# Expert weights of a mixture-of-experts layer read in place at a register-held address

## The chip, the cores and the metric

One core of a Trainium2 chip. The metric is the device time in microseconds of one execution; less is better. Engines are named PE (TensorE), DVE (VectorE), ACT (ScalarE), POOL (GpSimd) and SP (SyncE); "ACTq", "SPq" and the like are their instruction streams (DMA issues, register and semaphore instructions).

## What is computed

A network of five stages over x of shape (32, 64, 16, 16): a positional term, a linear attention with a small convolution, a causal pooling over the batch, a mixture of experts, a second linear attention, a second mixture of experts. The change touches the two mixtures alone. Each takes 8192 tokens of 64 numbers:

```python
logits = einsum('bsd,de->bse', x, gate_w) + gate_b         # 16 experts
top_probs, top_idx = top_k(softmax(logits), 2)             # two per token, renormalised
h1 = einsum('bsd,edh->bseh', x, w1)                        # 64 -> 128, per expert
h2 = einsum('bsd,edh->bseh', x, w2)
hidden = silu(h1) * h2
expert_out = einsum('bseh,eho->bseo', hidden, w3)          # 128 -> 64
out = einsum('bseo,bse->bso', expert_out, dispatch)
```

All is float32. Matrix products are made of two terms, a value rounded to fp32r and the rest that the rounding leaves.

## The kernel before

The kernel computes only the two chosen experts of each token. Tokens are split into two parts (PARTS = 2) of 4096. For a part, the routing finds each token's two experts and a slot for each choice; slots are grouped in blocks of 256 (BS), and each block belongs to one expert. 24 units (NU) of two blocks (UNIT = 2) always hold them all. `owner` is a small integer tile in SBUF with the expert of each block. GpSimd scatters the tokens of a part to a DRAM buffer by slot (64 indirect DMAs, line 980) and later gathers the results (64, line 992).

All weights of all 16 experts lie in one SBUF tile, `WR` of [128, 16, 320] float32: per expert 128 columns of w1, 128 of w2, 64 of w3. Which expert a unit needs is known only at run time. So SP, for each unit, reads the two owners from `owner` into registers (line 964; one load of two numbers, each then checked against 0 and 15), and issues two DMAs that copy the two experts' [128, 320] from `WR` to a ring of four, `wb` (line 967). It may do so once VectorE has finished with that buffer (`w_lo`, four units before).

The loop over units is a software pipeline written out by hand (`steps`): eight units written out, twelve in a loop of four per turn whose index is in a register, the last four written out. Step n does on each engine, in this order:

- ScalarE: issue the load of unit n+4's tokens from DRAM into `xb` (line 1107); weights of n+3: wait for the fetched weights, copy `wb` to `wr[..., 0]`, rounded (line 1102, semaphore `w_hi`); tokens of n+3: copy the transposed tokens out of PSUM (line 1113); silu of n+2 (line 1118); halve n+1: round the hidden values (line 1124); issue the store of n-1's result (line 1128).
- VectorE: result of n-1 (reduction, line 1272); weights of n+3: wait for `w_hi`, subtract `wr[..., 0]` from `wb` to get the rest (line 1249, `w_lo`); product of n+2 (line 1256); rest of n+1 (line 1262).
- TensorE: transpose the tokens of n+3 (line 1033), the two up products of n+2 (line 1049), the down product of n (line 1060).

`xb`, `wb`, `wr` and `yb` are rings of four units; `xt`, `gate`, `hid`, `hh`, `hlo` and the PSUM banks are rings of two.

Around the loops: in the first mixture, both parts are routed, then GpSimd scatters part 0 and part 1, and after that gathers part 0. ScalarE starts the loop of part p when `scattered[p]` is full. After both loops VectorE combines part 0 (line 1309 and 1310); part 1's gather runs in the next stage. In the second mixture, part 0 was routed and scattered in the stage before; part 1 is routed first, then both loops run beside the scatter of part 1 and the gather of part 0. The last stage gathers part 1 and writes the output. Stages are separated by a barrier of all engines.

Of the kernel before, what the change touches and what calls it, by code (L numbers as in the profile page):

```python
# [16 lines left out]
F32 = mybir.dt.float32  # L17
# [7 lines left out]
P = 128  # L25
# [817 lines left out]
class Mixture:  # L843
# [53 lines left out]
    def blocks_room(self, st, sem, outlives):  # L897

        def sb(name, shape, dt=F32):
            return st.enter_context(self.nc.sbuf_tensor(self.L + name, shape, dt))  # L900

        def sems(*names):
            return [sem(self.L + n) for n in names]
        self.GY = [(outlives or st).enter_context(self.nc.sbuf_tensor(f"{self.L}gy{h}", [P, 2, TH, C], F32))
                   for h in range(PARTS - 1)] + self.GY[-1:]
        self.xb = sb("xb", [P, 4, 4, P])
        self.xt = sb("xt", [P, 2, UNIT * BS], F32R)
        self.wb = sb("wb", [P, 4, UNIT, WC])
        self.wr = sb("wr", [P, 4, 2, UNIT, WC], F32R)
        self.gate = sb("gate", [P, 2, UNIT * BS])  # L910
        self.hid = sb("hid", [P, 2, UNIT * BS])
        self.hh = sb("hh", [P, 2, UNIT * BS], F32R)
        self.hlo = sb("hlo", [P, 2, UNIT * BS], F32R)
        self.yb = sb("yb", [P, 4, 4 * C])
        self.own_v, = sems("ov")
        self.x_in, self.w_in, self.stored = (sems(*(f"{n}{j}" for j in range(4))) for n in ("xl", "wl", "ys"))
        self.turned, self.xt_out, self.up1, self.up2, self.down = sems("bt", "bx", "b1", "b2", "bd")
        self.w_hi, self.w_lo, self.silu, self.prod, self.h_hi, self.h_lo, self.y_out = sems(
            "wh", "wo", "si", "pr", "hh_", "ho", "yo")
# [36 lines left out]
                     ).then_inc(self.g_loaded, 16)  # L956

    def sync(self, sp):
        for part in range(PARTS):
            def fetch(n, j, i):  # L960

                self.free(sp, self.w_lo, part, n, 4)
                owners = self.owner[0:1, part, bass.ds(n, 1)].rearrange("p n b -> p (n b)")
                _, experts = self.nc.values_load_multi_w_load_instructions(
                    owners, engines=[mybir.EngineType.SP], min_val=0, max_val=E - 1)
                for b in range(UNIT):
                    sp.dma_start(self.wb[:, j, b:b + 1], self.WR[:, bass.ds(experts[b], 1)]).then_inc(self.w_in[j], 16)
            sp.wait_ge(self.owned, part + 1)
            self.steps(sp, fetch)
        for j in range(4):  # L970

            sp.wait_ge(self.stored[j], 16 * PARTS * ((NU + 3 - j) // 4))

    def scatter(self, pool, part):

# [117 lines left out]
        act.wait_ge(self.exp_in, part + 1)  # L1093
        act.activation(self.mx[:, part, 3], self.mx[:, part, 2], ACT.Exp).then_inc(self.exp_out, 1)

    def scalar(self, act):
        ps = self.ps
        for part in range(PARTS):
            def weights(n, j, i):
                act.wait_ge(self.w_in[j % 4], UNIT * self.filled(part, j, i))  # L1100
                self.free(act, self.down, part, n, 4)
                act.copy(self.wr[:, j % 4, 0], self.wb[:, j % 4]).then_inc(self.w_hi, 1)  # L1102

            def load(n, j):

# [137 lines left out]
    def vector(self, dve, then):  # L1243
        ps = self.ps
        for part in range(PARTS):
            def weights(n, j):

                dve.wait_ge(self.w_hi, part * NU + n + 1)
                dve.tensor_tensor(self.wr[:, j % 4, 1], self.wb[:, j % 4], self.wr[:, j % 4, 0].bitcast(F32),  # L1249
                                  ALU.subtract).then_inc(self.w_lo, 1)  # L1250

            def product(n, j):
                dve.wait_ge(self.silu, part * NU + n + 1)
# [59 lines left out]
def stage_mixture(nc, sem, mix, first, ready, weights_in, outlives=None):  # L1313


    with ExitStack() as st:
# [6 lines left out]
        with nc.Block() as block:  # L1323
            @block.sync
            def _(sp):
                if not first:
                    mix.load_gate(sp)
                sp.wait_ge(*weights_in)
                mix.sync(sp)

            @block.gpsimd
            def _(pool):
                pool.wait_ge(*ready)
                for part in range(first, PARTS):
                    mix.scatter(pool, part)
                for part in range(PARTS - 1):
                    mix.gather(pool, part)

            @block.tensor
            def _(pe):  # L1340
                for part in range(first, PARTS):
                    mix.route_tensor(pe, part)
                mix.tensor(pe)

            @block.scalar
            def _(act):
                for part in range(first, PARTS):
                    mix.route_scalar(act, part)
                mix.scalar(act)

            @block.vector
            def _(dve):
                then = counter(dve, mix.own_v)
                for part in range(first, PARTS):
                    mix.route_vector(dve, then, part, (lambda: None) if part else (lambda: mix.split_gate(dve)))
                mix.vector(dve, then)
                if outlives is None:
                    for part in range(PARTS - 1):
                        mix.combine(dve, then, part)
# [448 lines left out]
```

## Time and profile before

| What | us |
|---|---|
| runs (three) | 1463.96, 1475.67, 1478.31 |
| median of the runs | 1475.67 |
| span of the profiled execution, first to last instruction | 1099.1 |
| PE busy in the span | 602.3 |
| DVE busy | 698.3 |
| POOL busy | 589.1 |
| ACT busy | 410.9 |
| mean granted TensorE clock | 0.753 |

The profile is one execution. Its page gives the span from the first to the last instruction, not the time of the whole execution; the runs' times hold what lies around the span too. A row of the timeline gives start, duration, engine, line, operation and tiles, and in brackets the idle time before it with what ended it. The four expert loops lie at about 364 to 440 and 451 to 530 us (first mixture), 824 to 909 and 921 to 998 us (second).

### The profile page before, as it was taken

What the parts mean: (1) busy time and instruction counts of PE and PEld (TensorE: products, weight loads), DVE (VectorE), ACT (ScalarE), POOL (GpSimd) and SP (SyncE); (2) the same over time, 40 slices, a digit from 0 to 9 for tenths busy, and PEclk for the clock granted to TensorE, in tenths of its full rate; (3) what the DMA queues carried; (4) which work ended last, traced back from release to release, by engine and by line L of the source; (5) the groups of instructions that cost most, each with busy time, mean ns of one, the idle gap of its engine ahead of it and who ended that gap; (6) DMA issues with size and microseconds to landing.
All of it is one profiled execution on the core that took longest, in us unless ns stands there. A gap on an engine that the chain in (4) does not pass through costs nothing. (4 is left out here: it accounts for less than half of the span.)

```text
span 1099.1 us, 12315 instructions
## 1 busy us (share of the span) xinstructions
PE 602.3 (55%) x3397; PEld 478.4 (44%) x3397; DVE 698.3 (64%) x1125; ACT 410.9 (37%) x688; POOL 589.1 (54%) x558
## 2 busy tenths in 40 slices
PE   2789776213310588477279841598155884783000
PEld 2774773213310587477144431244044774772000
DVE  6482474686670598478877589775458893885111
ACT  1454225131300576467224232143135773771000
POOL 0242141420777778777477600677205777775775
PEclk9979887555555799699679865698557996996555
DMA  3000991000211698688261100011104985882211
GB/s 106 7 1 1 207 354 25 0 1 0 94 46 52 198 292 243 198 249 241 57 103 24 24 1 0 38 46 53 53 22 147 299 259 185 261 250 62 55 35 38
DMA packets 126199, 118.91 MB, mean 108 GB/s; under 512 B 24917, under 2 KB 111525, under 8 KB 126147
## 3 DMA queue, kind: packets, MB, share of 16 engines
q1 hardware_dynamic: 56104, 54.93, 16.5%
q10 hardware_dynamic: 53659, 38.16, 11.9%
q0 software_dynamic: 16384, 25.20, 8.4%
q8 instruction: 23, 0.38, 0.1%
q14 instruction: 29, 0.24, 0.1%
HBM read 42.73 MB, written 44.04 MB: 79 GB/s over the span
## 5 line engine op out<-in xcount | busy, mean ns | idle before, releaser
L980 POOL DMA_INDIRECT blocks_x<-L_ffnmhl,L_ffnslot x192 | 198.5, 1034 | 162.9 <-DVE L_ffnslot L1233 105.0
L992 POOL DMA_INDIRECT gy_last<-blocks_y,L_ffnslot x128 | 129.7, 1013 | 57.0 <-issue 38.4
L992 POOL DMA_INDIRECT L_ffngy<-blocks_y,L_ffnslot x128 | 128.1, 1001 | 39.0 <-issue 39.0
L1033 PE MATMUL L_ffnps<-ident,L_ffnxb 128*128 128x128 f32 x384 | 65.5, 300 | 128.3 <-DMA L_ffnxb<-blocks_x 118.6
L1249 DVE TENSOR_TENSOR L_ffnwr<-L_ffnwb,L_ffnwr 128x640 fp32r<-128x640 f32 x96 | 79.2, 826 | 69.7 <-ACT L_ffnwr L1102 68.9
L1049 PE MATMUL L_ffnps<-L_ffnxt,L_ffnwr 128*128 128x256 f32 x768 | 118.3, 299 | 3.0 <-ACT L_ffngate L1118 2.4
L980 POOL DMA_INDIRECT blocks_x<-L_ffnlhl,L_ffnslot x64 | 66.3, 1036 | 82.3 <-DVE L_ffnslot L1233 63.1
L1102 ACT CAST L_ffnwr<-L_ffnwb 128x640 fp32r<-128x640 f32 x96 | 69.8, 727 | 108.5 <-issue 86.5
L1033 PEld LDWEIGHTS L_ffnps<-ident,L_ffnxb 128*128 128x128 f32 x384 | 44.7, 151 | 138.7 <-issue 107.8
L1049 PEld LDWEIGHTS L_ffnps<-L_ffnxt,L_ffnwr 128*128 128x128 f32 x768 | 101.4, 197 | 4.5 <-issue 3.2
L1060 PE MATMUL L_ffnps<-L_ffnwr,L_ffnhlo 128*128 128x128 f32 x384 | 92.8, 280 | 0.0
L1060 PE MATMUL L_ffnps<-L_ffnwr,L_ffnhh 128*128 128x128 f32 x384 | 88.6, 268 | 6.6 <-DVE L_ffnhlo L1262 6.2
L1256 DVE TENSOR_TENSOR L_ffnhid<-L_ffngate,L_ffnps 128x512 f32<-128x512 f32 x96 | 65.5, 686 | 34.4 <-ACT L_ffngate L1118 31.6
L1060 PEld LDWEIGHTS L_ffnps<-L_ffnwr,L_ffnhh 128*128 128x128 f32 x384 | 74.7, 195 | 8.7 <-issue 6.9
L1537 ACT CAST l_vh<-l_vg 128x512 fp32r<-128x512 f32 x64 | 39.6, 619 | 98.2 <-DVE l_vg L1597 98.2
L1060 PEld LDWEIGHTS L_ffnps<-L_ffnwr,L_ffnhlo 128*128 128x128 f32 x384 | 75.0, 195 | 0.0
L1113 ACT CAST L_ffnxt<-L_ffnps 128x512 fp32r<-128x512 f32 x96 | 56.2, 585 | 48.3 <-PE L_ffnps L1033 40.8
L1472 PE MATMUL l_ps<-l_xT,l_wv 128*128 128x512 f32 x128 | 71.7, 652 | 1.2
L1006 PE MATMUL L_ffnps<-ident,L_ffnmhl 128*128 128x128 f32 x96 | 22.5, 428 | 90.0 <-DVE L_ffnmhl L1175 66.6
L1272 DVE TENSOR_REDUCE L_ffnyb<-L_ffnps 128x256 f32<-128x512 f32 x96 | 65.8, 685 | 3.7 <-PE L_ffnps L1060 3.5
L1597 DVE SCALAR_TENSOR_TENSOR l_vg<-l_ps,lw_bv,l_gain 128x512 f32<-128x512 f32 x64 | 48.0, 751 | 29.7 <-PE l_ps L1472 29.7
L1262 DVE TENSOR_TENSOR L_ffnhlo<-L_ffnhid,L_ffnhh 128x512 fp32r<-128x512 f32 x96 | 66.2, 689 | 0.4
(289 smaller groups left out, 1387.4 us busy)
## 6 DMA issues: line engine op xcount, KB each, us to landing
L_ffnwb<-WR SPq DMA_DIRECT2D x192, 160.0 KB, 3.4
L_ffnxb<-blocks_x ACTq DMA_DIRECT2D x96, 256.0 KB
blocks_x<-zeros SPq DMA_DIRECT2D x2, 6144.0 KB, 29.9
blocks_y<-L_ffnyb ACTq DMA_DIRECT2D x96, 128.0 KB
WR<-in_L_ffn_w SPq DMA_DIRECT2D x10, 512.0 KB, 11.0
blocks_x<-L_ffnmhl,L_ffnslot POOLq DMA_INDIRECT x192, 2.2
Xc<-in_x SPq DMA_DIRECT2D x4, 512.0 KB, 7.5
L_ffngy<-blocks_y,L_ffnslot POOLq DMA_INDIRECT x128
```

The lines of the kernel that those rows point to most:

```text
L980: pool.indirect_dma_start(self.XD[part], bass.IndirectOffsetOnAxis(self.slot[:, part, k, t:t + 1], 0), self.HL[part][:, t].rearrange("p a ...
L992: pool.indirect_dma_start(self.GY[part][:, k, t], None, self.YD[part], bass.IndirectOffsetOnAxis(self.slot[:, part, k, t:t + 1], 0)).then_ ...
L1033: ins = pe.transpose(ps[:, j % 2, s * P:(s + 1) * P], self.xb[:, j % 4, s], K["ident"][:])
L1049: ins = pe.matmul(ps[:, bank + j % 2, slots], self.wr[:, j % 4, k, b, c0:c0 + HID], x[:, slots], start=(k == 0), stop=(k == 1))
L1060: ins = pe.matmul(o, h[:, j % 2, s * P:(s + 1) * P], self.wr[:, j % 4, :, s * P // BS, 2 * HID:WC], start=(k == 0), stop=(k == 1))
L1102: act.copy(self.wr[:, j % 4, 0], self.wb[:, j % 4]).then_inc(self.w_hi, 1)
L1113: act.copy(self.xt[:, j % 2], ps[:, j % 2, :]).then_inc(self.xt_out, 1)
L1249: dve.tensor_tensor(self.wr[:, j % 4, 1], self.wb[:, j % 4], self.wr[:, j % 4, 0].bitcast(F32), ALU.subtract).then_inc(self.w_lo, 1)
L1256: dve.tensor_tensor(self.hid[:, j % 2], self.gate[:, j % 2], ps[:, 4 + j % 2, :], ALU.mult).then_inc(self.prod, 1)
L1262: dve.tensor_tensor(self.hlo[:, j % 2], self.hid[:, j % 2], self.hh[:, j % 2].bitcast(F32), ALU.subtract).then_inc(self.h_lo, 1)
L1272: dve.tensor_reduce(self.yb[:, j % 4].rearrange("p (s c) -> p s c", c=C), y, AX.X, ALU.add).then_inc(self.y_out, 1)
L1472: pe.matmul(ps[:, n % 2, :], wv[:, h].rearrange("p a c -> p (a c)"), xT[:, BC * (k % KP):BC * (k % KP + 1)].rearrange("p b n -> p (b n)"), ...
```

## The change

The ring `wb`, its semaphores and SP's whole fetch loop are gone. ScalarE and VectorE each read the two owners of a unit into registers of their own, and take the expert's weights straight from `WR` at an address computed from the register. Since the two experts of a unit do not lie side by side in `WR`, the copy and the subtraction are each done in two instructions of [128, 320] where there was one of [128, 640]. The semaphore `w_hi` is raised by the second copy, `w_lo` by the second subtraction. ScalarE's copy no longer waits for fetched weights, only for `down` of four units before; the waits for `owned` and for the weights' arrival from DRAM move from SP to ScalarE and VectorE.

```diff
@@ blocks_room
-        self.wb = sb("wb", [P, 4, UNIT, WC])
@@ sync
-        for part in range(PARTS):
-            def fetch(n, j, i):
-
-                self.free(sp, self.w_lo, part, n, 4)
-                owners = self.owner[0:1, part, bass.ds(n, 1)].rearrange("p n b -> p (n b)")
-                _, experts = self.nc.values_load_multi_w_load_instructions(
-                    owners, engines=[mybir.EngineType.SP], min_val=0, max_val=E - 1)
-                for b in range(UNIT):
-                    sp.dma_start(self.wb[:, j, b:b + 1], self.WR[:, bass.ds(experts[b], 1)]).then_inc(self.w_in[j], 16)
-            sp.wait_ge(self.owned, part + 1)
-            self.steps(sp, fetch)
+    def experts(self, engine, part, n):
+
+        owners = self.owner[0:1, part, bass.ds(n, 1)].rearrange("p n b -> p (n b)")
+        _, found = self.nc.values_load_multi_w_load_instructions(owners, engines=[engine], min_val=0, max_val=E - 1)
+        return [self.WR[:, bass.ds(e, 1)] for e in found]
@@ scalar
+        act.wait_ge(*weights_in)
         for part in range(PARTS):
+            act.wait_ge(self.owned, part + 1)
+
             def weights(n, j, i):
-                act.wait_ge(self.w_in[j % 4], UNIT * self.filled(part, j, i))
+                w = self.experts(mybir.EngineType.Activation, part, n)
                 self.free(act, self.down, part, n, 4)
-                act.copy(self.wr[:, j % 4, 0], self.wb[:, j % 4]).then_inc(self.w_hi, 1)
+                for b in range(UNIT):
+                    ins = act.copy(self.wr[:, j % 4, 0, b:b + 1], w[b])
+                ins.then_inc(self.w_hi, 1)
@@ vector
         for part in range(PARTS):
+            dve.wait_ge(self.owned, part + 1)
+
             def weights(n, j):
 
+                w = self.experts(mybir.EngineType.DVE, part, n)
                 dve.wait_ge(self.w_hi, part * NU + n + 1)
-                dve.tensor_tensor(self.wr[:, j % 4, 1], self.wb[:, j % 4], self.wr[:, j % 4, 0].bitcast(F32),
-                                  ALU.subtract).then_inc(self.w_lo, 1)
+                for b in range(UNIT):
+                    ins = dve.tensor_tensor(self.wr[:, j % 4, 1, b:b + 1], w[b], self.wr[:, j % 4, 0, b:b + 1].bitcast(F32),
+                                            ALU.subtract)
+                ins.then_inc(self.w_lo, 1)
```

## Rows read from the trace of the kernel before

**Rows 1.** busy time by stretch, the last expert loop: stretch, its length, engines, clock, DMA

```profile
921.00:997.00 76.00, 61.03 (x480) 58.06 (x480) 63.49 (x96) 54.09 (x96) 58.28 (x59) 0.95 0.77 230
```

**Rows 2.** instructions of line 1102 in each loop's steady part, first and last start

```profile
L1102 ACT CAST L_ffnwr<-L_ffnwb x21: 720/727/735, 374.3 to 432.1; 128x640 fp32r<-128x640 f32 x21
L1102 ACT CAST L_ffnwr<-L_ffnwb x21: 721/726/735, 459.4 to 520.7; 128x640 fp32r<-128x640 f32 x21
L1102 ACT CAST L_ffnwr<-L_ffnwb x21: 719/727/735, 843.0 to 900.2; 128x640 fp32r<-128x640 f32 x21
L1102 ACT CAST L_ffnwr<-L_ffnwb x21: 721/727/736, 929.0 to 988.7; 128x640 fp32r<-128x640 f32 x21
```

**Rows 3.** timeline of VectorE, 379 to 384: start, duration, operation

```profile
380.38 0.82 DVE L1249 TENSOR_TENSOR L_ffnwr<-L_ffnwb,L_ffnwr 128x640 fp32r<-128x640 f32 x1
381.11 0.68 DVE L1256 TENSOR_TENSOR L_ffnhid<-L_ffngate,L_ffnps 128x512 f32<-128x512 f32 x1
...
382.31 0.69 DVE L1272 TENSOR_REDUCE L_ffnyb<-L_ffnps 128x256 f32<-128x512 f32 x1
382.91 0.82 DVE L1249 TENSOR_TENSOR L_ffnwr<-L_ffnwb,L_ffnwr 128x640 fp32r<-128x640 f32 x1
```

**Rows 4.** timeline of ScalarE, 419 to 423

```profile
420.03 0.73 ACT L1102 CAST L_ffnwr<-L_ffnwb 128x640 fp32r<-128x640 f32 x1 [0.68 <-PE L_ffnps L1033]
...
420.94 0.40 ACTq L1128 DMA_DIRECT2D blocks_y<-L_ffnyb  x1
...
421.51 0.38 ACTq L1107 DMA_DIRECT2D L_ffnxb<-blocks_x  x1
421.63 0.62 ACT L1124 CAST L_ffnhh<-L_ffnhid 128x512 fp32r<-128x512 f32 x1
422.14 0.73 ACT L1102 CAST L_ffnwr<-L_ffnwb 128x640 fp32r<-128x640 f32 x1
```

**Rows 5.** who waited for whom: total us, times, longest

```profile
PE L_ffnps L1033 <- DMA L_ffnxb<-blocks_x: 118.6, 59, 48.2
```

**Rows 6.** timeline around the ends of the first layer's two loops

```profile
440.08 0.38 ACTq L1128 DMA_DIRECT2D blocks_y<-L_ffnyb  x1
...
449.19 1.95 ACTq L1107 DMA_DIRECT2D L_ffnxb<-blocks_x  x4
...
529.44 0.68 DVE L1309 TENSOR_TENSOR L_ffngy<-L_ffngy,L_ffnmx 128x512 f32<-128x512 f32 x1
```

**Rows 7.** timeline around the ends of the second layer's two loops

```profile
905.69 3.43 ACTq L1128 DMA_DIRECT2D blocks_y<-L_ffnyb  x3
...
918.62 1.95 ACTq L1107 DMA_DIRECT2D L_ffnxb<-blocks_x  x4
...
994.26 3.27 ACTq L1128 DMA_DIRECT2D blocks_y<-L_ffnyb  x3
...
999.78 0.95 POOL L992 DMA_INDIRECT L_ffngy<-blocks_y,L_ffnslot  x1 [0.30 <-issue]
```

**Rows 8.** DMA issues by line: count, size of one, us to landing

```profile
L_ffnwb<-WR SPq DMA_DIRECT2D x192, 160.0 KB, 3.4
```

**Rows 9.** instructions of line 964 on SP: duration ns min/median/max

```profile
L964 SPq TENSOR_LOAD <-L_ffnowner x96: 469/805/1912, 279.6 to 979.5; - x96
```

**Rows 10.** timeline of SP, first fetches, around 285 us

```profile
284.87 0.49 SPq L967 DMA_DIRECT2D L_ffnwb<-WR  x1
...
286.54 0.50 SPq L967 DMA_DIRECT2D L_ffnwb<-WR  x1
```

**Rows 11.** timeline of ScalarE, 403 to 406

```profile
403.31 0.60 ACT L1118 ACTIVATE L_ffngate<-L_ffnps 128x512 f32<-128x512 f32 x1
...
404.09 0.52 ACTq L1107 DMA_DIRECT2D L_ffnxb<-blocks_x  x1
404.71 0.73 ACT L1102 CAST L_ffnwr<-L_ffnwb 128x640 fp32r<-128x640 f32 x1 [0.29 <-issue]
...
405.82 0.60 ACT L1118 ACTIVATE L_ffngate<-L_ffnps 128x512 f32<-128x512 f32 x1
```

More of the change, by code:

```diff
@@ L915, in blocks_room @@
         self.own_v, = sems("ov")
-        self.x_in, self.w_in, self.stored = (sems(*(f"{n}{j}" for j in range(4))) for n in ("xl", "wl", "ys"))
+        self.x_in, self.stored = (sems(*(f"{n}{j}" for j in range(4))) for n in ("xl", "ys"))
         self.turned, self.xt_out, self.up1, self.up2, self.down = sems("bt", "bx", "b1", "b2", "bd")
@@ L1094, in route_scalar, with scalar @@
         act.activation(self.mx[:, part, 3], self.mx[:, part, 2], ACT.Exp).then_inc(self.exp_out, 1)
-    def scalar(self, act):
+    def scalar(self, act, weights_in):
         ps = self.ps
+        act.wait_ge(*weights_in)
         for part in range(PARTS):
+            act.wait_ge(self.owned, part + 1)
             def weights(n, j, i):
-                act.wait_ge(self.w_in[j % 4], UNIT * self.filled(part, j, i))
+                w = self.experts(mybir.EngineType.Activation, part, n)
                 self.free(act, self.down, part, n, 4)
-                act.copy(self.wr[:, j % 4, 0], self.wb[:, j % 4]).then_inc(self.w_hi, 1)
+                for b in range(UNIT):
+                    ins = act.copy(self.wr[:, j % 4, 0, b:b + 1], w[b])
+                ins.then_inc(self.w_hi, 1)
             def load(n, j):
@@ L1327, in _ @@
                     mix.load_gate(sp)
-                sp.wait_ge(*weights_in)
                 mix.sync(sp)
@@ L1348, in _ @@
                     mix.route_scalar(act, part)
-                mix.scalar(act)
+                mix.scalar(act, weights_in)
             @block.vector
```

## The prediction

> **What bounds the kernel now.** I began with the busy time per engine and stretch. In the four expert loops (24 units each; two parts in each of two mixture layers) no engine is full: in the last of them VectorE is busy 63.5 of 76 us, TensorE 61.0, ScalarE 54.1, at a granted clock of 0.95, so TensorE runs near its 2.4 GHz level [rows 1]. Next comes the period of a unit, from the starts of ScalarE's weight copy (line 1102): 57.8, 61.3, 57.2 and 59.7 us for 20 steps in the four loops, 236.0 us over 80 steps, 2.95 us a unit [rows 2]. Two floors lie beneath it. VectorE can repeat its four instructions in 382.91 - 380.38 = 2.53 us [rows 3]. ScalarE's shortest step is 422.14 - 420.03 = 2.11 us [rows 4]. What holds the period over both is the tokens' load: TensorE waited 118.6 us, 59 times, for `xb`, a few long waits at the start of parts among them [rows 5].
>
> Then the ends of the loops, since only there does the period become time of the kernel. In the first layer ScalarE issued the last store of part 0 at 440.08 (+0.38) and could not load part 1 until 449.19, when the scatters on GpSimd had ended: 8.7 us of slack. The end of part 1 has none: VectorE goes over to the combine without a pause, at 529.44 [rows 6]. In the second layer part 0 ended at 905.69 + 3.43 = 909.12 and part 1 began at 918.62: 9.5 us of slack. Part 1's last stores were issued by 997.53, the last gather of part 0 at 999.78 (+0.95) [rows 7]. With the landing of the stores still to come I take 1 us of slack there, of 0 to 3.2.
>
> **What the change takes away.** 192 transfers of 160 KB [rows 8], 30.7 MB, and ScalarE's and SP's waits around the staging tile. SP is on no path that sets the end, so its 96 register loads are worth nothing where they were. The transfers could at most quicken the tokens' load. That can bring the period from 2.95 down to VectorE's 2.53 and no lower, and in both parts 0 GpSimd's scatter holds the start of part 1 in any case. So the largest gain is 61.3 - 50.6 = 10.7 us in the first layer's part 1, and 1 us or less in the last, where the gather is last [rows 2, 3, 6, 7].
>
> **What it adds.** The 96 register loads now run twice, once in ScalarE's and once in VectorE's instruction stream. On SP one is a TENSOR_LOAD of 469/805/1912 ns (shortest, median, longest) [rows 9], followed by the checks of both numbers against 0 and 15 and by the addresses. SP's issue of one transfer ends at 284.87 + 0.49 = 285.36, the next unit's begins at 286.54 [rows 10]: 1.18 us for one load and its checks. With the shortest load, 0.47 to 0.48, that leaves about 0.65 us for checks and address (the first gap between instructions taken in), so a typical one costs 0.80 + 0.65 = 1.45 us; the bounds are 0.47 + 0.65 = 1.12 and 1.91 + 0.65 = 2.56, the latter never on average. I take the median and not the minimum, because on ScalarE the load stands right behind the issue of the tokens' load, with transfers in flight. Each engine also runs two instructions of 128x320 for one of 128x640. ScalarE's 128x640 takes 727 ns and its 128x512 0.62 us, so a fixed part of about 0.19 us, of which 0.11 overlaps (the 0.62 us instruction at 421.63 lets the next start 0.51 later): +0.08 us [rows 2, 4]. VectorE's are alike: 0.82 us, with the next instruction 0.73 later [rows 3].
>
> **Where it lies on ScalarE.** In a step ScalarE's stream goes: copy, tokens, silu, halve, the store's DMA issue, the load's DMA issue, then the next copy. The DMA issues run in the sequencer while the datapath still works: the store's starts at 420.94, well before halve does at 421.63, and the load's ends at 421.51 + 0.38 = 421.89 [rows 4]. The register load comes right behind that, ahead of the copy. So the period becomes: 1.86 us from the copy's start to the end of the load's issue, 1.45 for the register load with checks, 0.10 to the copy's start (as in [rows 11], below), 0.08 for the split: 3.5 us, 0.55 more than now. This assumes that the sequencer can go ahead as in these rows. The other pattern stands beside it: where silu starts at 403.31 the next does at 405.82, 2.51 us, and the load's issue ends at 404.09 + 0.52 = 404.61, 0.10 before the copy at 404.71 [rows 11]; there all of 1.45 + 0.08 is added and the period is 4.0 us. I take 3.5, because the slow pattern appears where tokens wait for TensorE, and at 3.5 us TensorE and the tokens' transfer have time to spare.
>
> **Where it lies on VectorE.** Its load comes behind `result` and before the wait for ScalarE's rounded copy. The datapath still has a subtraction and the reduction to run then (the reduction at 382.31 holds it 0.60 us, the subtraction before it has the same size) [rows 3], and ScalarE's own load, as long, goes on meanwhile. I cost it at nothing: 2.53 + 0.08 plus what sticks out, at most 0.3 to 0.5 us, stays under 3.5. The cover is gone if the load cannot start before the reduction has finished; that is a rival below. Queued behind it are both weight subtractions, then product, for which ScalarE's halve and so the store wait.
>
> **The sum.** In the prologue of a part three copies stand in a row; I count two loads as exposed, 2.9 us; the first hides behind the tokens' first transfer. Against the profiled span, per part: 20 x 3.5 = 70.0 us less the old 20 steps, plus 2.9. First layer, part 0: 12.2 + 2.9 - 8.7 slack = 6.4. Part 1: 8.7 + 2.9 = 11.6. Second layer, part 0: 12.8 + 2.9 - 9.5 = 6.2. Part 1: 10.3 + 2.9 - 1 = 12.2. Together +36.4 us: a span of 1135.5 for 1099.1. The page gives this execution's span and not its whole time; the median of the runs is 1475.67, so 376.6 us lie around the span, and I leave those as they are. 1475.7 + 36.4 = 1512 us.
>
> **Rivals.**
> *The load is longer or the stream waits (4.0 us a unit).* ScalarE stays in the pattern of [rows 11]. Per part: 80.0 less the old steps, plus 2.9: 25.1 - 8.7, 21.6, 25.7 - 9.5, 23.2 - 1: +76 us, 1552. For it: steps look so now. Against it: what made them so goes away.
> *The load on VectorE waits for its datapath.* Then a cycle on VectorE is 0.60 to the reduction, 0.69 for it, 1.45 for the load, 0.81 for two subtractions, 0.60 for product: 4.15 us. Per part 83.0: 28.1 - 8.7, 24.6, 28.7 - 9.5, 26.2 - 1: +88 us, 1564. No row shows a register load on an engine with a datapath, so only its absence speaks for it.
> *The loads are hidden (not slower by what can be told).* A sequencer that runs further ahead than in [rows 4] would dispatch silu and halve at once and be bound by its own sum: two DMA issues of about 0.5 with their registers, 1.45 for the load, some 0.5 for the rest, 3.0 us. That gives 5.1 - 8.7 (so nothing), 1.6, nothing, 2.2: +4 us, 1479. It decides as soon as the period stays under 3.2 us, where the sum falls to about +15.
> The Trainium skill (Advanced Engine Details and Errata, Sequencer and Instruction Queues) says that engine instructions can be queued while the sequencer executes a control instruction, with a queue of eight on ScalarE and VectorE. By that rule the result is this third rival, 1479; the trace agrees that DMA issues run under the datapath's work, but no row shows more than two instructions queued.
> *Faster.* The gain bounded above, 12 us at the most, needs loads at no cost. It is under 1%.
>
> **How the numbers follow.** The forecast (3.2 to 3.8 us a unit, 1488 to 1536) gets 0.47, the 4.0 us stream 0.17, VectorE's wait 0.13, hidden loads 0.20, anything faster 0.03. I can tell from no change about 1%, 15 us. The range reaches from between the hidden case and the forecast's low end, 1486, to above both slow rivals, 1575. Slower by over 1% takes the forecast nearly whole and both slow rivals: 0.75; within 1%: 0.22; faster: 0.03.
>
> **What would show it.** Period of the copy's starts 3.4 to 3.6 us in all four loops; TENSOR_LOAD on ScalarE and VectorE with a median of 0.6 to 0.9 us; the copy twice, at a little over half of 727 ns; TensorE's wait for `xb` nearly gone inside the loops; ScalarE idle before the copy by over 1 us with the reason "issue"; the gap of 8.7 us between the parts of the first layer closed. It would be wrong if the load is much cheaper on these engines, if a wait on w_hi or silu doubles the cost by coupling the two streams, or if TensorE, idle more, is granted the 1.2 GHz level in the loops: they now run at 0.95 [rows 1].

## The result, and the profile after

| | before | after |
|---|---|---|
| median | 1476.04 us (4 runs, 1463.96 to 1478.31) | 1495.23 us (4 runs, 1493.99 to 1501.02) |
| ratio, 95% interval | | 1.0157 (1.011 to 1.0204) |
| profiled execution | span 1099.1 us | span 1492.2 us, in a run of 1493.99 us |

The change costs 1.6% by that ratio and 1.3% by the medians. The ratios in this document compare only runs within 1.5% of the fastest of their kernel, the medians are over all runs. The prediction said 1512 us; the time is inside its range and on its side, at 19 us more where 36 were forecast. Much of what follows is about why the size was half, and about the last line of the table: the two profiled executions are 393 us apart, the runs 19.

The loads of the look-ups in the profiled execution of after, by line (duration ns shortest/median/longest):

```profile
L965 ACTq TENSOR_LOAD <-L_ffnowner x96: 488/518/778, 373.8 to 1387.5; - x96
L965 DVEq TENSOR_LOAD <-L_ffnowner x96: 523/529/775, 386.0 to 1388.5; - x96
```

The weight copies and subtractions of after, as groups (busy us and mean ns, then idle us before them by releaser):

```profile
L1100 ACT CAST L_ffnwr<-WR 128x320 fp32r x192 | 78.7, 456 | 247.2 <-remote 128.8 <-issue 112.2 <-PE L_ffnps L1054 6.2
L1252 DVE TENSOR_TENSOR L_ffnwr<-WR,L_ffnwr 128x320 fp32r<-128x320 f32 x192 | 86.0, 489 | 52.4 <-ACT L_ffnwr L1100 34.6 <-issue 16.0
```

The loads are shorter than the 469/805/1912 ns of [rows 9], and narrow: the median is almost the shortest. The copy has 128.8 us of idle time put down to "remote", a reason that the page of before does not have at all. The busy time of after by stretch says more (columns: stretch, its length, busy us of PE, PEld, DVE, ACT, POOL with instructions, granted clock, DMA share, GB/s):

```profile
380.00:465.00 85.00, 19.86 (x92) 16.99 (x92) 17.23 (x31) 12.03 (x23) 63.81 (x64) 0.54 0.20 60
465.00:527.00 62.00, 48.80 (x340) 42.66 (x340) 46.62 (x85) 40.49 (x88) 0.12 (x1) 0.89 0.39 110
```

Both lines are one expert loop. While GpSimd scatters (64 indirect transfers in 85 us) TensorE and VectorE are busy for about a fifth of the time and ScalarE for a seventh. When it has nothing to do they run at full pace, for the last 17 or so of the 24 units. In [rows 1], of the recorded execution of before, GpSimd was busy 58.28 of 76 us and VectorE 63.49 beside it. Which of the two differences is the change's was the first thing to settle.

### The profile page after: what moved, and what is told of

It reads as the page before. It is cut to its first block and busy times, and to the rows that moved or that the text cites. A ratio compares the mean times of both kernels' runs of the same rounds, so it can differ in the third digit from the quotient of the medians.

```text
span 1492.2 us, 12846 instructions
## 1 busy us (share of the span) xinstructions
PE 673.1 (45%) x3397; PEld 513.1 (34%) x3397; DVE 710.8 (48%) x1222; ACT 418.6 (28%) x785; POOL 570.2 (38%) x558
## 5 line engine op out<-in xcount | busy, mean ns | idle before, releaser
L1043 PE MATMUL L_ffnps<-L_ffnxt,L_ffnwr 128*128 128x256 f32 x768 | 131.0, 320 | 173.3 <-ACT L_ffnxt L1112 86.4
L1043 PEld LDWEIGHTS L_ffnps<-L_ffnxt,L_ffnwr 128*128 128x128 f32 x768 | 112.5, 217 | 190.7 <-issue 93.6
L1054 PE MATMUL L_ffnps<-L_ffnwr,L_ffnhh 128*128 128x128 f32 x384 | 104.4, 303 | 127.1 <-DVE L_ffnhlo L1266 110.3
L1100 ACT CAST L_ffnwr<-WR 128x320 fp32r x192 | 78.7, 456 | 247.2 <-remote 128.8
L1475 PE MATMUL l_ps<-l_xT,l_wv 128*128 128x512 f32 x128 | 86.0, 769 | 68.1 <-DVE l_vg L1600 42.5
L974 POOL DMA_INDIRECT blocks_x<-L_ffnlhl,L_ffnslot x64 | 63.4, 991 | 136.2 <-DVE L_ffnslot L1232 117.0
L1252 DVE TENSOR_TENSOR L_ffnwr<-WR,L_ffnwr 128x320 fp32r<-128x320 f32 x192 | 86.0, 489 | 52.4 <-ACT L_ffnwr L1100 34.6
L1054 PE MATMUL L_ffnps<-L_ffnwr,L_ffnhlo 128*128 128x128 f32 x384 | 103.1, 300 | 0.0
L1054 PEld LDWEIGHTS L_ffnps<-L_ffnwr,L_ffnhlo 128*128 128x128 f32 x384 | 83.1, 216 | 0.0
L1117 ACT ACTIVATE L_ffngate<-L_ffnps 128x512 f32<-128x512 f32 x96 | 57.3, 599 | 56.5 <-remote 41.4
L1488 PE MATMUL l_ps<-l_vh,l_pw 128*128 128x512 f32 x64 | 66.6, 1040 | 0.0
```

The lines of the kernel that those rows point to most:

```text
L974: pool.indirect_dma_start(self.XD[part], bass.IndirectOffsetOnAxis(self.slot[:, part, k, t:t + 1], 0), self.HL[part][:, t].rearrange("p a ...
L1043: ins = pe.matmul(ps[:, bank + j % 2, slots], self.wr[:, j % 4, k, b, c0:c0 + HID], x[:, slots], start=(k == 0), stop=(k == 1))
L1054: ins = pe.matmul(o, h[:, j % 2, s * P:(s + 1) * P], self.wr[:, j % 4, :, s * P // BS, 2 * HID:WC], start=(k == 0), stop=(k == 1))
L1100: ins = act.copy(self.wr[:, j % 4, 0, b:b + 1], w[b])
L1117: act.activation(self.gate[:, j % 2], ps[:, 2 + j % 2, :], ACT.Silu).then_inc(self.silu, 1)
L1252: ins = dve.tensor_tensor(self.wr[:, j % 4, 1, b:b + 1], w[b], self.wr[:, j % 4, 0, b:b + 1].bitcast(F32), ALU.subtract)
```

## The experiments

In what follows a stall is a stretch of several to tens of us in which ScalarE or VectorE stands still inside an expert loop while GpSimd issues its transfers. The runs fell on four chips, of two kinds: on two of them before takes 1099 us (chips without the stalls), on two 1468 to 1484 us (chips with the stalls). Each chip served one group of runs, so whether the chip or the moment makes the kind is not shown; "kind of chip" stands for either. Times are compared only within a chip. Steps are 20 copies of ScalarE to a loop as in [rows 2], summed over the four loops.

**Before, once more.** No edit.

> The kernel before, once more, unchanged, for its trace. The changed kernel's profiled execution has a span of 1492.2 us in a run of 1493.99, so nearly all its time is inside the span; the recorded execution of before has a span of 1099.1 us against runs of 1476. Theory (that execution was unlike the runs): the span is about 1474 us, and the trace shows stalls of 5 to 50 us in the expert loops, as the changed kernel's does, in which ScalarE or VectorE waits for a count of TensorE that was due long before. Rival (the 377 us lie outside the span, as the prediction took it): the span is again near 1099 us, no such stalls, and the changed kernel lost 393 us inside its span and won 374 outside.

The run took 1095.25 us with a span of 1093.6, on a chip where 23 runs of before have a median of 1099.63. So neither theory holds as put: the recorded execution of before was no odd one, and under 2 us lie outside the span. It must have been taken on a chip without the stalls, and the 1475.67 us on one with them. The runs of before beside p_move, below, show the latter from inside: one of 1466.06 us has a span of 1464.4. The steps repeat those of before, 235.5 us for 236.0.

**No look-up.** All units take experts 0 and 1:

```
-        _, found = self.nc.values_load_multi_w_load_instructions(...)
-        return [self.WR[:, bass.ds(e, 1)] for e in found]
+        return [self.WR[:, b:b + 1] for b in range(UNIT)]
```

> The changed kernel without its register loads: every unit uses the weights of experts 0 and 1, so its output is not the reference's; all else stands. It leaves out 96 loads with their checks on ScalarE and 96 on VectorE. Theory A (the loads on ScalarE set the extra time, as in the prediction's sum): the steady period of the weight copy falls from the 3.1 to 3.4 us of the changed kernel to about 2.7 to 2.9, and the time falls by about 19 us, to that of before, 1476, or a little lower. Theory B (the loads lie under other work; the extra comes from the split instructions or from where the stalls fall): the time stays within 6 us of 1495.

1092.65 us for 1099.63, ratio 0.9942 (0.9921 to 0.9964). VectorE's timeline (start, duration):

```profile
399.55 0.69 DVE L1274 TENSOR_REDUCE L_ffnyb<-L_ffnps 128x256 f32<-128x512 f32 x1
400.15 0.89 DVE L1250 TENSOR_TENSOR L_ffnwr<-WR,L_ffnwr 128x320 fp32r<-128x320 f32 x2
400.95 0.68 DVE L1258 TENSOR_TENSOR L_ffnhid<-L_ffngate,L_ffnps 128x512 f32<-128x512 f32 x1
401.55 0.69 DVE L1264 TENSOR_TENSOR L_ffnhlo<-L_ffnhid,L_ffnhh 128x512 fp32r<-128x512 f32 x1
402.15 0.69 DVE L1274 TENSOR_REDUCE L_ffnyb<-L_ffnps 128x256 f32<-128x512 f32 x1
402.75 0.89 DVE L1250 TENSOR_TENSOR L_ffnwr<-WR,L_ffnwr 128x320 fp32r<-128x320 f32 x2
```

From subtraction to subtraction 2.60 us without a pause: VectorE's floor, [rows 3] with the split in it. The 80 steps take 213.0 us (2.66 each). Theory A, and with the staging gone the period falls under that of before, by 0.28 us. The steps lose 22.5 us in all and the time only 7, about what the first layer's part 1 alone loses (52.2 us for 60.4): the gain of both parts 0 goes into the wait for the scatters.

**The look-ups added to before**, their values unused, the staging and its transfers as they were:

```
             def weights(n, j, i):
+                w = self.experts(mybir.EngineType.Activation, part, n)
                 act.wait_ge(self.w_in[j % 4], UNIT * self.filled(part, j, i))
...
             def weights(n, j):
+                w = self.experts(mybir.EngineType.DVE, part, n)
                 dve.wait_ge(self.w_hi, part * NU + n + 1)
```

> The kernel before (staging tile, transfers and 128x640 instructions as they were) with the same register loads and checks added on ScalarE and VectorE, their values unused. Theory A: the added loads alone cost what the change costs, +15 to +25 us over before, with a period of 3.1 to 3.4 us. Theory B (the loads are covered by the datapath's work): within 6 us of before. If the transfers of the weights mattered too, this kernel would be slower than the changed one, because it has both.

1118.28 us, ratio 1.0187 (1.0149 to 1.0225); the steps take 267.2 us, 3.34 each. Theory A. Its ratio is above the change's own on such a chip (1.0057, below), so the staging matters too. Its loads and, of the first loop, its weight copies, by line:

```profile
L977 DVEq TENSOR_LOAD <-L_ffnowner x96: 524/656/1444, 320.4 to 1002.5; - x96
L977 ACTq TENSOR_LOAD <-L_ffnowner x96: 492/840/1649, 361.5 to 1001.5; - x96
L964 SPq TENSOR_LOAD <-L_ffnowner x96: 468/851/1499, 276.1 to 992.3; - x96
...
L1111 ACT CAST L_ffnwr<-L_ffnwb x21: 725/727/735, 371.6 to 439.9; 128x640 fp32r<-128x640 f32 x21
```

On ScalarE a load costs 840 ns here and 533 in the changed kernel on such a chip (a_third). The instruction is the same; what differs is the staging: its transfers, and SP's own look-ups in the same tile, which are the third row and [rows 9] again. Which of the two lengthens the load no run tells.

**The split alone**: two copies and two subtractions of 128x320, from the staging tile.

```
-                act.copy(self.wr[:, j % 4, 0], self.wb[:, j % 4]).then_inc(self.w_hi, 1)
+                for b in range(UNIT):
+                    ins = act.copy(self.wr[:, j % 4, 0, b:b + 1], self.wb[:, j % 4, b:b + 1])
+                ins.then_inc(self.w_hi, 1)
```

> The kernel before with only the split: ScalarE and VectorE run two instructions of 128x320 for each of 128x640, from the staging tile. The changed kernel's rows give 456 ns for ScalarE's copy with the second starting 0.36 us behind the first, so some 0.08 us more for each unit, and as much on VectorE. Theory A: 96 units x 0.08 = 8 us at most, part of it under the tokens' load, so 0 to +8 us over before. Theory B (the split is the cause of the 19 us, over the read-write bubble of each instruction and its wait): +15 us or more.

1096.66 us, ratio 0.9991 (0.9963 to 1.0019), steps 235.4 us. The split costs nothing that can be told. Theory A, at its lower end.

**The change again**, no edit, on either kind of chip.

> The changed kernel, unchanged, once more. In the first group of runs before took 1476 and the change 1495 us; in the last group before took 1099.6 us with a span of 1093.6 and none of the long stalls. Theory A (the change's cost is in the steady steps of the loops and has nothing to do with the stalls): here too it is +15 to +22 us over before, 1115 to 1122, with a period of 3.1 to 3.4 us as in e2_loads (267 us over 80 steps, against 236). Theory B (the transfers taken away pay for part of the loads): the period is 3.0 to 3.2 and the time +5 to +14 us. Theory C (the 19 us come from where the stalls fall): within 5 us of before.

It fell on a chip with the stalls: 1502.77 for 1483.87 us, 1.0125 (1.0089 to 1.016), theory A's time.

> The changed kernel once more, as the measure for the two edits that run with it. There are two kinds of measurement by now: before at 1476 to 1484 us, with 12 to 65 us stalls in the first steps of each loop, and before at 1099.6 without them. If this one is of the second kind: Theory A (the cost lies in the steady steps, 2.95 to about 3.15 us): 80 steps x 0.2 = 16 us, less what the slack after both parts 0 takes (8.7 and 9.5), plus two exposed look-ups for each prologue, so +5 to +14 us over before and under e2_loads's +18.7. Theory B (the cost is bound to the stalls): within 4 us of before. If of the first kind: +15 to +22 us again.

On a chip without them: 1105.41 for 1098.68 us, 1.0057 (1.0028 to 1.0086), theory A again. So the change costs 1.3 to 1.6% on one kind of chip and 0.6% on the other, and the cost doesn't need the stalls. Its 6.7 us and the period of 3.12 us, next, are also what a_again's theory B had: the transfers taken away pay for part of the loads. The weight copies of a_third in the steps of the four loops, by line (in three of the windows the last start is that of the second copy of a pair, 0.36 us later):

```profile
L1100 ACT CAST L_ffnwr<-WR x41: 452/458/470, 372.3 to 435.7; 128x320 fp32r x41
L1100 ACT CAST L_ffnwr<-WR x42: 453/457/471, 459.8 to 521.8; 128x320 fp32r x42
L1100 ACT CAST L_ffnwr<-WR x42: 452/458/469, 846.8 to 909.9; 128x320 fp32r x42
L1100 ACT CAST L_ffnwr<-WR x42: 452/458/468, 933.1 to 995.1; 128x320 fp32r x42
```

63.4 + 61.6 + 62.7 + 61.7 = 249.4 us: 3.12 a unit, for 2.95. Next, ScalarE's timeline where part 1 of the first layer begins, in a_third (the first loads of the tokens):

```profile
447.88 1.95 ACTq L1106 DMA_DIRECT2D L_ffnxb<-blocks_x  x4
```

And in a_again, with part 0's last stores ahead of them:

```profile
532.78 2.93 ACTq L1127 DMA_DIRECT2D blocks_y<-L_ffnyb  x3
535.83 2.00 ACTq L1106 DMA_DIRECT2D L_ffnxb<-blocks_x  x4
```

In the first the scatters hold the load until 447.88, as in [rows 6]. In the second the load follows the stores at once, 532.78 + 2.93 = 535.71, then 535.83: the scatters were over at 463.9 and there is no slack.

**One half at a time.** ScalarE in place, VectorE from the staging tile:

```
-                act.wait_ge(self.w_in[j % 4], UNIT * self.filled(part, j, i))
-                act.copy(self.wr[:, j % 4, 0], self.wb[:, j % 4]).then_inc(self.w_hi, 1)
+                w = self.experts(mybir.EngineType.Activation, part, n)
+                for b in range(UNIT):
+                    ins = act.copy(self.wr[:, j % 4, 0, b:b + 1], w[b])
+                ins.then_inc(self.w_hi, 1)
...
             def weights(n, j, i):
+                dve.wait_ge(self.w_in[j % 4], UNIT * self.filled(part, j, i))
```

> Half of the change: ScalarE looks the experts up and copies from the weights in place, in two instructions; VectorE still subtracts from the staging tile, 128x640, and the sync queue still fills it. Theory A (the load on ScalarE, in a row with its two DMA issues, is what lengthens the step): this half costs nearly all, +14 to +19 us over before, with a period of 3.2 to 3.4. Theory B (it takes both loads, because VectorE waits for w_hi after its own): +0 to +8 us.

1521.04 us for 1483.87, 1.026 (1.0225 to 1.0294): 18 us more than the whole change, and more than theory A. Its load, where the first loop runs without stalls:

```profile
L977 ACTq TENSOR_LOAD <-L_ffnowner x16: 634/792/1357, 475.8 to 526.4; - x16
```

The changed kernel's (a_again) there, on the same chip:

```profile
L965 ACTq TENSOR_LOAD <-L_ffnowner x17: 493/529/643, 473.0 to 523.1; - x17
```

VectorE in place, ScalarE from the staging tile:

```
+                w = self.experts(mybir.EngineType.DVE, part, n)
                 dve.wait_ge(self.w_hi, part * NU + n + 1)
-                dve.tensor_tensor(self.wr[:, j % 4, 1], self.wb[:, j % 4], ...
+                for b in range(UNIT):
+                    ins = dve.tensor_tensor(self.wr[:, j % 4, 1, b:b + 1], w[b], ...
```

> The other half: VectorE looks the experts up and subtracts from the weights in place, in two instructions; ScalarE still copies from the staging tile, 128x640, and the sync queue fills it. Theory A (VectorE's load lies under its datapath's work and under ScalarE's copy): within 5 us of before, with a period of 2.9 to 3.0. Theory B (VectorE has the most work and its load is exposed): +10 us or more, with a period of 3.2 or more, and no overlap of the load with the reduction before it.

1495.99 us for 1483.87, 1.009 (1.006 to 1.012): theory B's time, with about theory A's period (medians of a loop's 20 steps, 2.80 to 3.07 us). What of it is the look-up this run doesn't settle. Neither half has the gain of the change, since the staging stays for both.

**One look-up for four units**, eight numbers at a time (seven look-ups to a loop, not the six that the expectation says):

```
+            if j == 3:
+                held["loop"] = self.look_up(engine, part, n, 4)
+            return held["loop"][(j - 3) * UNIT:(j - 2) * UNIT]
```

> The changed kernel with the look-up for four units at a time on either engine: eight numbers in one look-up, six look-ups to a loop of 24 units for 24; the instructions on weights are those of the change. Theory A (each look-up costs a load of some 0.5 to 0.9 us that stops the stream, plus checks of 0.15 us a number): per unit 0.2 for 0.6 us of load and the same checks, so the period falls by 0.2 to 0.4 us from that of the changed kernel, 10 to 20 us of time: within 5 us of before or up to 5 below it, near e1_const's 0.994. Theory B (the checks and addresses are the cost and not the load): as the changed kernel, within 4 us.

1547.47 us, 1.0435 (1.0398 to 1.0472): both theories are wrong. Its load, by line:

```profile
L975 ACTq TENSOR_LOAD <-L_ffnowner x28: 551/818/1780, 373.5 to 1428.9; - x28
```

ScalarE's timeline around one of them:

```profile
520.59 0.38 ACTq L1117 DMA_DIRECT2D L_ffnxb<-blocks_x  x1
524.79 0.82 ACT L1111 CAST L_ffnwr<-WR 128x320 fp32r x2 [4.33 <-PE L_ffnps L1037]
```

Between the load's issue (done at 520.97) and the copy at 524.79 ScalarE's stream does nothing but look up: one load, then eight checks. Spread over four steps each look-up lies partly under the datapath's work; in one piece of 3.8 us it does not. VectorE has a piece of the same length of its own at the same time, and its subtraction also waits for ScalarE's copy.

**No bounds checks** (a number is a count clamped to 15):

```
-            ... engines=[engine], min_val=0, max_val=E - 1)
+            ... engines=[engine], min_val=0, max_val=E - 1, skip_runtime_bounds_check_because="...")
```

> The changed kernel without the checks of the looked-up numbers against 0 and 15 (a number here is a count clamped to 15, so it stays in bounds). In the changed kernel's trace a look-up on ScalarE takes 1.08 us from its first to its last instruction, of which the load is 0.49 and the two checks 0.47; on VectorE the checks are two of 190 ns and two of 23. Theory A (the whole look-up is on the path): the period falls by 0.2 to 0.4 us to 2.8 to 2.9, the time by 10 to 20 us, to before or below. Theory B (the period is set by VectorE's datapath, or by TensorE): within 4 us of the changed kernel.

1100.08 us for 1098.68, 1.0014 (0.9984 to 1.0043); steps 235.2 us, 2.94 each. Against the changed kernel on that chip, 1105.41, the checks were worth 5 us, and 0.18 us a unit: less than theory A's time, its mechanism nonetheless.

**VectorE's look-up ahead of result:**

```
             def step(n, j, i):
                 peeled = isinstance(n, int)
+                w = self.experts(mybir.EngineType.DVE, part, n + 3) if not peeled or n + 3 < NU else None
                 if peeled and n >= 1:
                     result(n - 1, (j + 3) % 4, (n - 1) // 4)
```

> The changed kernel with VectorE's look-up moved ahead of result in each step, so that product, rest and the reduction (some 0.6 us each) lie over it instead of rest and reduction; nothing else. Theory A (VectorE's look-up sticks out in every second step, as in the trace: reduction done at 502.80, subtraction begins at 503.58): the period falls by 0.2 to 0.3 us, the time by 8 to 18 us. Theory B (ScalarE's stream is the bound, 2.73 us from look-up to look-up at least, and VectorE only waits for its copy): within 4 us of the changed kernel.

1116.31 us, 1.0143 (1.0106 to 1.0179): slower than the change, against both theories. Steps 273.1 us, 3.41 each. VectorE's look-up in one step, by line:

```profile
L965 DVEq FUSED_REGOPS  x3: 57/190/190, 412.3 to 413.4; - x3
L965 DVEq TENSOR_LOAD <-L_ffnowner x1: 601/601/601, 412.4 to 412.4; - x1
```

Its timeline there:

```profile
411.82 0.69 DVE L1260 TENSOR_TENSOR L_ffnhid<-L_ffngate,L_ffnps 128x512 f32<-128x512 f32 x1
412.43 0.69 DVE L1266 TENSOR_TENSOR L_ffnhlo<-L_ffnhid,L_ffnhh 128x512 fp32r<-128x512 f32 x1
413.72 0.69 DVE L1276 TENSOR_REDUCE L_ffnyb<-L_ffnps 128x256 f32<-128x512 f32 x1 [0.61 <-issue]
```

The look-up's first register instruction began at 412.35, when product had been running for 0.5 us, and not when product was queued. Under it lay only rest, until 413.11; the reduction, which now stands behind the look-up, came 0.61 us late. What held the look-up shows on ScalarE, whose halve the rest ahead of it waits for:

```profile
411.68 0.62 ACT L1123 CAST L_ffnhh<-L_ffnhid 128x512 fp32r<-128x512 f32 x1
```

Halve ends at 412.30 and the look-up starts 0.05 us later. So it does in 68 of this run's 96 look-ups (0.04 or 0.05 us), however long product had been running by then. VectorE's stream did not go past rest before the data for rest were there, and the edit had moved the look-up right behind that wait. I had taken the stream to run further ahead.

**A candidate:** no checks, and the tokens' loads and the results' stores issued by the sync queue:

```
+    def sync(self, sp):
+        for part in range(PARTS):
+            def load(n, j):
+                self.free(sp, self.turned, part, n, 4)
+                sp.dma_start(self.xb[:, j % 4] ...
+            def store(n, j):
+                sp.wait_ge(self.y_out, part * NU + n + 1)
+                sp.dma_start(self.unit_rows(self.YD[part], n), ...
```

> A candidate that should beat both: the changed kernel without the bounds checks, and with the tokens' loads and the results' stores issued by the sync queue, which the change left empty; VectorE's look-up stands where the change has it. In p_nocheck ScalarE's stream holds, between the dispatch of silu and the next copy, two DMA issues of 0.40 us with 0.14 of registers each, and the look-up; VectorE's subtraction waited for that copy (copy done 493.92, subtraction at 494.06, the reduction done at 493.53). Theory A (ScalarE's copy comes late because of its DMA issues): the period falls from 2.94 to the 2.65 of e1_const, VectorE's own floor, and the time to 5 to 12 us under before on either kind of chip. Theory B (what is left is VectorE's look-up): as p_nocheck, within 4 us of before where before takes 1100, up to 5 above it where before takes 1480.

1456.42 us for 1468.36, both medians over all runs. The ratio is 1.0022 (0.9951 to 1.0093); it and the medians disagree because a single run of before at 1440.48 us leaves only 3 of its 17 in the ratio. So whether this version beats before is open. The median of a loop's 20 steps is 2.56 to 2.68 us in the four loops, theory A's figure, against 3.06 to 3.29 for the changed kernel (a_again) and 2.72 to 2.88 for p_nocheck on the other kind of chip, so part of the gain is the checks'.

## Why the prediction was right, and where its size came from

*Where the time is.* "376.6 us lie around the span, and I leave those as they are" was wrong. On the chips that were timed they lie inside the span. So a sum made on a span of 1099.1 was added to 1475.7, a time of other conditions. On a chip like that of the profile the change costs 0.6%, "within 1%" by the prediction's own cases. On the kind that was timed the traces show no slack to take off, and without it the prediction's own sum is 36.4 + 8.7 + 9.5 + 1 = 55.6 us, for 19 measured. That 36 came nearer is luck: slack taken off that isn't there made up for part of a step priced too high.

*The period.* 3.5 us were forecast, 3.12 measured (and 3.06 to 3.29 in the medians of a_again). Four kernels on chips without the stalls split this up, per unit, from 80 steps each:

| kernel | steps, us | per unit | difference |
|---|---|---|---|
| e3_split: staging, no look-up | 235.4 | 2.94 | |
| e1_const: no staging, no look-up | 213.0 | 2.66 | -0.28, staging gone |
| a_third: the change | 249.4 | 3.12 | +0.46, look-ups |
| e2_loads: staging and look-ups | 267.2 | 3.34 | +0.22, staging back |

Each figure is one trace; three kernels that should agree (before, e0_before, e3_split) give 236.0, 235.5 and 235.4 us. a_third ran on another chip than the other three.

The look-ups cost 0.46, or 0.40 beside the staging (267.2 - 235.4); the prediction had 0.47 for them and 0.08 for the split. The term that failed is the other one: "the transfers could at most quicken the tokens' load", bounded, and then put at nothing. It is worth 0.22 to 0.28 us a unit, 18 to 22 us over the steps, where the staging is its transfers, ScalarE's wait for them and SP's look-ups together; no run parts these. That the transfers are the larger part is likely and not shown: in e0_before's loops the DMA engines are busy for 0.84 to 0.94 of the time, in a_third's for 0.56 to 0.58 (the stretches in the last section). The prediction had the reason in its hands: it named the tokens' load as what holds the period above VectorE's 2.53 us [rows 3, 5]. It then built the new period from ScalarE's stream as [rows 4] shows it with the staging in place.

*The load's price.* 0.80 us were taken, 0.53 measured; 0.65 for checks and address, about 0.7 measured. ScalarE's timeline in the changed kernel (a_again):

```profile
501.01 0.39 ACTq L1106 DMA_DIRECT2D L_ffnxb<-blocks_x  x1
502.61 0.82 ACT L1100 CAST L_ffnwr<-WR 128x320 fp32r x2 [1.23 <-issue]
503.14 0.40 ACTq L1127 DMA_DIRECT2D blocks_y<-L_ffnyb  x1
503.34 0.58 ACT L1112 CAST L_ffnxt<-L_ffnps 128x512 fp32r<-128x512 f32 x1
503.72 0.40 ACTq L1106 DMA_DIRECT2D L_ffnxb<-blocks_x  x1
503.81 0.60 ACT L1117 ACTIVATE L_ffngate<-L_ffnps 128x512 f32<-128x512 f32 x1
504.30 0.62 ACT L1123 CAST L_ffnhh<-L_ffnhid 128x512 fp32r<-128x512 f32 x1
505.34 0.82 ACT L1100 CAST L_ffnwr<-WR 128x320 fp32r x2 [0.41 <-issue]
```

From the end of the load's issue to the copy 502.61 - 501.40 = 1.21 us, of which the load is 0.5. The median of [rows 9] was that of a load beside the staging, and the change takes the staging away: p_act, with it, has 792 ns where the change has 529 on the same chip. The prediction's shortest load, 0.47, would have been nearer than its median.

*How far ScalarE runs ahead.* The prediction took 1.86 us from the copy to the end of the load's issue, as in [rows 4]. Here it is 504.12 - 502.61 = 1.51: the store's issue at 503.14 comes before tokens, silu and halve have begun. So the rival with hidden loads had the mechanism nearly right, 2.73 us in this step, while ScalarE still stood idle 0.41 and 1.23 us. The Trainium skill (Advanced Engine Details and Errata, Sequencer and Instruction Queues) has instructions queued while the sequencer goes on, up to eight; on ScalarE the trace agrees, with three seen. On VectorE one instruction is seen queued, in the rows below: the look-up's load at 505.2 starts before the reduction that stands ahead of it, at 505.74. That p_early's look-up came late is no sign of a shorter lead; it stood behind a wait that was not yet met.

*VectorE.* That its load doesn't wait for the datapath was right, and the rival at 4.15 us falls. Its loads in the same stretch of a_again, by line:

```profile
L965 DVEq TENSOR_LOAD <-L_ffnowner x2: 527/534/541, 502.2 to 505.2; - x2
```

And its timeline:

```profile
502.12 0.69 DVE L1276 TENSOR_REDUCE L_ffnyb<-L_ffnps 128x256 f32<-128x512 f32 x1
503.58 0.89 DVE L1252 TENSOR_TENSOR L_ffnwr<-WR,L_ffnwr 128x320 fp32r<-128x320 f32 x2 [0.78 <-ACT L_ffnwr L1100]
...
505.74 0.68 DVE L1276 TENSOR_REDUCE L_ffnyb<-L_ffnps 128x256 f32<-128x512 f32 x1
```

The load at 502.2 runs beside the reduction of 502.12. VectorE stands idle for 0.78 us behind it, but that is ScalarE's doing: VectorE's own look-up was over at 503.28 and the copy only at 503.43. "I cost it at nothing" was nearly right for all of the change: in a_third VectorE stood idle before its subtractions for 92.8 us in the 64 steps in which ScalarE's copy came last, and for 7.3 us in the 19 in which its own look-up did. So p_early, whose theory A took this idle time for VectorE's, moved a look-up that was hardly on the path.

*The slack.* On chips without the stalls the 8.7 us after the first part 0 come again: in e0_before the last stores end at 432.36 + 2.93, the loads begin at 444.03. With the measured steps the prediction's own sum gives 63.4 - 57.8 + 2.9 - 8.7 (so nothing), 61.6 - 61.3 + 2.9 = 3.2, 62.7 - 57.2 + 2.9 - 9.5 (nothing), and 61.7 - 59.7 + 2.9 - 1 = 3.9: 7.1 us, for 6.7 between the medians. That these two meet is in part luck, since the traces bear out only some of the terms. That both parts 0 cost nothing holds: in a_third the wait for the scatters is still there after them, though shorter.

```profile
441.25 2.93 ACTq L1127 DMA_DIRECT2D blocks_y<-L_ffnyb  x3
...
1000.38 3.85 ACTq L1127 DMA_DIRECT2D blocks_y<-L_ffnyb  x3
...
1007.81 0.95 POOL L986 DMA_INDIRECT L_ffngy<-blocks_y,L_ffnslot  x1 [0.30 <-issue]
```

From 444.18 to the loads at 447.88 there are 3.7 us. The prologue's 2.9 us is too much where it counts, in both parts 1: from the first load of the tokens to the fourth weight copy a_third takes 459.8 - 447.9 = 11.9 us, before 459.4 - 449.2 = 10.2, and in the second layer 11.4 against 10.4. All of part 1 of the first layer, from its first load to its last reduction, takes 81.7 us, for 80.3 and 79.5 in the two traces of before: 1.4 to 2.2 us more. And the last loop does not end the second layer: its stores are issued by 1004.23, the last gather ends at 1008.76, and in e0_before too the gather is 6 us behind the stores. What ends that layer is GpSimd's scatter of part 1 and gather of part 0 in a row, 167.7 and 171.8 us in the two traces of before and 175.0 in a_third; whether the change has a part in that, three single traces can't tell. With the stalls there is no slack, so the same steps give 249.4 - 236.0 + 4 x 2.9 = 25 us; 19 were measured, both in the result and in a_again. That this is where the 12 us between the kinds come from is argued from the lack of slack. No trace of before with the stalls was taken, and the first units of each loop there are paced by GpSimd and not by these steps, which may be the 6 us too many, as may the 2.9 us of the prologue.

*TensorE's clock* played no part on the chips without the stalls: it is granted 0.97 to 1.00 in the steady steps of e0_before's loops and of a_third's (the stretches in the last section). On those with the stalls it is granted 0.54 to 0.56 while GpSimd issues and 0.87 to 0.95 after, in the changed kernel; what before has there no trace shows.

*The signs that the prediction named.* The period was 3.12 and not 3.4 to 3.6, the load's median 0.53 and not 0.6 to 0.9, and the gap between the first layer's parts shrank to 3.7 us on one kind of chip and is not there on the other. The copy came as said, at 458 ns for over half of 727.

## What to carry over

Ask first whether the profiled execution and the timed runs are the same thing: if span and time differ by more than a few us, they come from different conditions, and slack read from the one can't be spent in the other. When a transfer is removed, price the operations that stay by what they cost without it, here a register load of 0.53 us for 0.80, and give the stage that waited for the same transfers its gain. A look-up in an engine's stream costs its load and its checks wherever the datapath has less queued than that; spread them, leave out checks that the data make needless, and before moving one look at which wait will stand ahead of it: behind a wait that is met late it starts late, whatever work is queued.

## What the runs showed of the hardware that I had not expected

The two kinds of chip differ in one thing above all: whether other engines go on while GpSimd issues indirect transfers. The same program, the first layer's loops by stretch (columns as above), on a chip without the stalls (a_third):

```profile
372.00:436.00 64.00, 55.30 (x401) 48.68 (x401) 54.47 (x101) 46.45 (x101) 50.04 (x46) 0.97 0.58 169
460.00:521.00 61.00, 53.62 (x396) 46.90 (x396) 53.52 (x99) 45.91 (x100) 47.71 (x44) 1.00 0.56 150
```

Before on such a chip (e0_before), for the clock and the share of the DMA engines:

```profile
369.00:427.00 58.00, 47.14 (x391) 45.03 (x391) 51.88 (x80) 45.53 (x81) 44.88 (x44) 1.00 0.91 281
454.00:515.00 61.00, 49.10 (x399) 47.19 (x398) 52.41 (x81) 46.21 (x82) 46.67 (x48) 0.97 0.84 250
```

And the change on a chip with them (a_again):

```profile
380.00:465.00 85.00, 18.92 (x92) 16.33 (x92) 15.94 (x30) 12.03 (x23) 64.03 (x64) 0.56 0.20 61
465.00:527.00 62.00, 50.89 (x346) 44.73 (x347) 47.49 (x87) 41.05 (x88) 0.00 (x0) 0.87 0.38 111
540.00:620.00 80.00, 14.10 (x68) 11.98 (x66) 8.36 (x16) 8.20 (x17) 59.98 (x63) 0.54 0.16 35
623.00:685.00 62.00, 52.32 (x362) 45.55 (x363) 49.92 (x91) 43.19 (x93) 0.00 (x0) 0.91 0.41 116
```

GpSimd's instructions take as long on both (the scatter of line 974 has a median of 968 and 971 ns). Up to the first of them the two traces are level: it starts at 272.1 us in a_third and at 271.0 in a_again. In the stalls looked at, an engine waits for a count of TensorE that should be there. In a_again's timeline the last matmul of a `down` ends at 441.34 + 0.41 = 441.75. VectorE's reduction and ScalarE's copy, which both wait for it, start 18 us later and within 0.1 us of each other, near the end of the scatters (the last at 462.9). ScalarE's look-up for that copy had been over since 428.7:

```profile
441.34 0.41 PE L1054 MATMUL L_ffnps<-L_ffnwr,L_ffnhlo 128*128 128x128 f32 x1
...
460.03 0.69 DVE L1276 TENSOR_REDUCE L_ffnyb<-L_ffnps 128x256 f32<-128x512 f32 x1 [20.35 <-issue]
460.12 0.82 ACT L1100 CAST L_ffnwr<-WR 128x320 fp32r x2 [32.59 <-issue]
```

Why the two kinds differ no run tells. That the stalls aren't the change's is shown by p_act and p_dve, which keep the staging and have them too; before's own times there, with a span as long as the run (1464.4 of 1466.06 us), fit that. Of the 395 us between the spans of a_third and a_again nothing lies before GpSimd's first of 512 indirect transfers, and some 300 lie in the four expert loops beside them.
